# The prologue of a two-layer transformer kernel: tables for four batches first, rounding shared out, FiLM weights in three pieces

## The reference

```python
ln    = (x - mean) / sqrt(var + 1e-5) * ln_g + ln_b
gamma = cond @ Wg.T + bg ;  beta = cond @ Wb.T + bb        # one row for each batch
h     = gamma * ln + beta
q,k,v = h @ Wqkv.T + bqkv                                  # 16 heads of 32
out   = (softmax(q k^T) / sqrt(512)) v ;  out = out @ Wp.T + bp
h1    = out + x ;  x1 = gamma*LN(h1)+beta + h1             # the same gamma, beta
```

## Time and profile before

| what | us |
|---|---|
| median of 3 runs | 1538.35 (1538.13 to 1538.81) |
| the profiled execution, its own time | 1537.32 |
| its span in the profile | 1535.4 |
| TensorE busy in the span | 1515.0 |
| TensorE busy from 0 to 28.67 us | 13.33 |
| first `scores` matmul starts | 53.20 |

### The profile page before, as it was taken

The page is one execution under the profiler, slowest core; times in us unless marked ns, Lnnn a source line. Parts: engine busy times, 40 slices in busy tenths (PEclk is TensorE's granted clock), DMA queues, the critical chain, the costliest instruction groups (busy, mean ns, idle before and its releaser), DMA issues.

```text
span 1535.4 us, 24533 instructions
## 1 busy us (share of the span) xinstructions
PE 1515.0 (99%) x8992; PEld 1235.9 (80%) x8992; DVE 788.4 (51%) x1616; ACT 592.9 (39%) x1884; POOL 581.4 (38%) x504
## 2 busy tenths in 40 slices
PE   5999999999999999999999999999999999999999
PEld 4888888888887668888788888888888888888887
DVE  5677777777766675555546342332524233252522
ACT  4656565656554446555554221211212121121210
POOL 5656666676654545443553311021211102121100
PEclk9999999999999999999999999999999999999999
DMA  7122222222126234333343220020201002020100
GB/s 252 63 80 87 80 93 77 96 77 91 58 81 232 71 138 158 97 103 126 122 127 114 69 69 15 1 82 0 75 7 68 14 1 81 0 75 7 55 1 28
DMA packets 60237, 117.87 MB, mean 77 GB/s; under 512 B 6352, under 2 KB 10448, under 8 KB 60144
## 3 DMA queue, kind: packets, MB, share of 16 engines
q1 hardware_dynamic: 60144, 116.65, 22.4%
HBM read 91.33 MB, written 25.30 MB: 76 GB/s over the span
## 4 chain that ended last, share of the span: by engine, by line
PE 97%; POOL 1%; DVE 1%; DMA 1%; SPq 0%; issue 0%
PE bank L587 27%; PE bank L589 27%; PE bank L588 27%; PE bank L666 4%; PE bank L659 2%; PE bank L677 2%; PE bank L963 2%; PE bank L884 1%; PE bank L718 1%; PE bank L709 1%; PE bank L611 1%; PE bank L987 1%; POOL xa L1746 1%; DMA xa<-xt_in 1%; PE bank L906 1%; PE bank L966 0%
## 5 line engine op out<-in xcount | busy, mean ns | idle before, releaser
L1705 DVE CAST g_hi<-gf 128x512 fp32r<-128x512 f32 x128 | 68.7, 537 | 427.1 <-ACT gf L1271 427.1
L1271 ACT ACTIVATE gf<-bank,cols 128x512 f32<-128x512 f32 x128 | 88.3, 690 | 512.6 <-PE bank L589 512.6
L1106 ACT ACTIVATE pa<-bank,neg_max 128x128 f32<-128x128 f32 x512 | 181.7, 408 | 135.5 <-DVE neg_max L1378 135.5
L587 PE MATMUL bank<-w_hi,g_hi 128*128 128x512 f32 x512 | 200.5, 392 | 0.0
L587 PE MATMUL bank<-hb_hi,w_hi 128*128 128x512 f32 x512 | 199.4, 389 | 0.3 <-DVE vb_lo L1294 0.3
L589 PE MATMUL bank<-w_hi,g_lo 128*128 128x512 f32 x512 | 199.4, 389 | 0.0
L588 PE MATMUL bank<-w_lo,g_hi 128*128 128x512 f32 x512 | 199.2, 389 | 0.0
L589 PE MATMUL bank<-hb_hi,w_lo 128*128 128x512 f32 x512 | 199.2, 389 | 0.0
L588 PE MATMUL bank<-hb_lo,w_hi 128*128 128x512 f32 x512 | 199.2, 389 | 0.0
L1781 POOL TENSOR_TENSOR pa<-pa,rec 128x512 f32<-128x512 f32 x128 | 143.2, 1126 | 56.2 <-DVE rec L1401 56.1
L1755 POOL TENSOR_TENSOR xrc<-xrc,b 128x512 f32<-128x512 f32 x32 | 48.7, 1550 | 303.0 <-DMA xrc<-x_dram 302.9
(11 more groups left out here) (201 smaller groups left out, 3132.6 us busy)
## 6 DMA issues: line engine op xcount, KB each, us to landing
rows<-st_dram SPq DMA_DIRECT2D x32, 512.0 KB, 4.3
xb<-x_dram SPq DMA_DIRECT2D x60, 256.0 KB, 2.9
xa<-xt_in SPq DMA_DIRECT2D x32, 256.0 KB, 4.4
xra<-xt_in SPq DMA_DIRECT2D x32, 256.0 KB, 2.7
x_dram<-h SPq DMA_DIRECT2D x32, 256.0 KB, 2.0
xrb<-x_dram SPq DMA_DIRECT2D x32, 256.0 KB, 3.3
stage_w<-w_in SPq DMA_DIRECT2D x16, 512.0 KB, 3.8
x_dram<-xrb SPq DMA_DIRECT2D x32, 256.0 KB, 2.2
```

What stands on the lines that cost most here:

```text
L587: nc.tensor.matmul(dst, w_hi, a_hi, start=start, stop=False)
L1106: last = nc.scalar.activation(pa[:, j, m, :], scores_bank[j][:, m * P:(m + 1) * P], ACT.Exp, bias=neg_max[:, j * C + m:j * C + m + 1], acc ...
L1271: nc.scalar.activation(gf[f % 2][:], bank[f % 2][:], ACT.Gelu, bias=cols[:, B1_COL + f:B1_COL + f + 1])\
L1705: nc.vector.tensor_copy(g_hi[:, r, :], gf[f % 2][:]).then_inc(g_hi_ready, 1)
```

## The change

Nothing is computed differently; order and engine change.

- SyncE issues the first three x tiles ahead of `cond`, the FiLM weights in three pieces (k = 0 and 1; k = 2; k = 3) with `cols` after the first, the fourth x tile behind them, x tiles 4 to 7 ahead of the bias rows, and waits for Wv's load on the new `wk_first` and on `wa_lo_made` 2 (Wp's: 3).
- VectorE makes first the `st_ln` of batches 0 to 3 alone (`first_tables`, 7 instructions of 128x16), and all the tables (`all_tables`, 8 instructions) only inside the loop at m = 0. `st_made` counts one more. TensorE's 8 transposes of the table (`table_rows`) move to m = 2, and VectorE's `st_rows` copies to m = 1.
- Of the first four batches VectorE rounds the two that it scales, ScalarE the other two; VectorE takes the four low halves after all four are rounded.
- GpSimd splits Wk's first 128 columns; ScalarE rounds Wq's first columns, then the rest of Wk, then of Wq.
- TensorE takes `queries(0, 0)` directly after `first_keys`, and each transpose of the next x tile between keys and queries.
- ScalarE's `copy_k(0, m + 1)` stands ahead of `scale_a(GB + m)`, and behind a wait for all the tables; the splits of Wv and Wp stand one round earlier, at m = 0 and 1, on ScalarE and VectorE.

```diff
+            for t in range(3):
+                load_x(t)
             sp.dma_start(cond[:], cond_t.rearrange("(k p) b -> p k b", p=P)).then_inc(consts_in, 16)
-            for t in range(2):
-                load_x(t)
-            for k in range(2):
+            for k in range(3):
+                piece = wgb_piece(k)
                 for i, w in enumerate((wg_t, wb_t)):
-                    sp.dma_start(wgb[:, i, 2 * k:2 * k + 2], weight(w[2 * k * P:2 * (k + 1) * P, :])).then_inc(wgb_in[k], 16)
-            for t in range(2, GB):
-                load_x(t)
+                    sp.dma_start(wgb[:, i, piece], weight(w[piece.start * P:piece.stop * P, :])).then_inc(wgb_in[k], 16)
+                if k == 0:
+                    sp.dma_start(cols[:], cols_d).then_inc(consts_in, 16)
+            load_x(3)
...
@@ TensorE
+            pe.wait_ge(wa_hi_made, 1)
+            pe.wait_ge(wa_lo_made, 1)
+            queries(0, 0)
+            for m in range(1, C):
+                if m == 1:
                     pe.wait_ge(wa_hi_made, 2)
                     pe.wait_ge(wa_lo_made, 2)
+                pe.wait_ge(k_copied, m)
+                keys(0, m)
+                if m > 1:
+                    pe.wait_ge(n_scaled_act, m + 1)
+                norm_a(GB + m - 1, x_bank)
...
+                if m == 2:
+                    table_rows()
+                pe.wait_ge(q_copied, m)
                 queries(0, m)
...
@@ ScalarE
             for n in range(0, GB, 2):
                 scale_a(n, (vq_bank, None, o_bank)[n])
-            for n in range(GB):
                 round_a(n)
-            split_wa(1)
+            split_wa(1, slice(0, P))
+            split_wa(0, slice(P, D))
+            split_wa(1, slice(P, D))
...
+            copy_k(0, 0)
+            act.wait_ge(st_made, 2)
             for m in range(C):
-                copy_k(0, m)
-                if 0 < m < 3:
-                    split_wa(m + 1)
+                if m + 1 < C:
+                    copy_k(0, m + 1)
                 scale_a(GB + m, x_bank)
                 round_a(GB + m)
+                if m < 2:
+                    split_wa(m + 2)
...
@@ VectorE
+            def first_tables():
+                def four(v):
+                    return cols[:, COL[v]:COL[v] + C].unsqueeze(2).broadcast_to([P, C, GB])
+                ga, be, sh = tmp_a[:, :, 0:GB], tmp_b[:, :, 0:GB], tmp_b[:, :, GB:2 * GB]
+                then(nc.vector.tensor_tensor(ga, ft[:, :, 0, 0, 0:GB], four("bg"), ALU.add))
...
+                nc.vector.tensor_tensor(st_ln[:, 0:GB, C:2 * C].rearrange("p b c -> p c b"), sh, be, ALU.add)\
+                    .then_inc(st_made, 1)
...
+                dve.wait_ge(n_scaled_dve, n // 2 + 1)
+                nc.vector.tensor_copy(h_hi[0][:, :, n * P:(n + 1) * P], h_full(n)).then_inc(hi_ready, 1)
-            split_wa(0, slice(0, P))
             for n in range(GB):
-                norm_low(n)
+                norm_low(n, GB)
+            split_wa(1, 1, slice(0, P))
             var_a(GB)
             mean_var(GB)
             add_eps(GB)
-            split_wa(1, slice(0, P))
-            split_wa(0, slice(P, D))
-            split_wa(1, slice(P, D))
...
+            split_wa(0, 2, slice(P, D))
+            split_wa(1, 3, slice(P, D))
...
             for m in range(C):
                 copy_q(0, m)
+                var_a(GB + m + 1)
+                mean_var(GB + m + 1)
+                add_eps(GB + m + 1)
+                if m == 0:
+                    all_tables()
+                if m == 1:
+                    dve.wait_ge(st0_t, 1)
+                    for i in range(2):
+                        nc.vector.tensor_copy(st_rows[:, i * D:(i + 1) * D], ps_t[i][0:NB, :]).then_inc(st_rows_made, 1)
                 norm_low(GB + m)
-                if m < 3:
-                    var_a(GB + m + 2)
-                    mean_var(GB + m + 2)
-                    add_eps(GB + m + 2)
-                if 0 < m < 3:
-                    split_wa(m + 1)
+                if m < 2:
+                    split_wa(m + 2, m + 4)
...
@@ GpSimd
+            for n in range(GB):
+                norm_a(n)
+            first = slice(0, P)
+            pool.wait_ge(stage_in[0], 16)
+            nc.gpsimd.tensor_copy(wk_hi[:, :, first], stage_a[:, 0, :, first]).then_inc(wk_first, 1)
+            pool.wait_ge(wk_first, 1)
+            nc.gpsimd.tensor_tensor(wk_lo[:, :, first], stage_a[:, 0, :, first], wk_hi[:, :, first].bitcast(F32),
+                                    ALU.subtract).then_inc(wk_first, 1)
```

More of the change, by code:

```diff
@@ L301, in block_pair_kernel @@
         var2_ready, ln2_shifted, x1_ready = sem("var2_ready"), sem("ln2_shifted"), sem("x1_ready")
-        raw_in = [sem(f"raw_in{i}") for i in range(4)]
+        raw_in = [sem("raw_vp_in"), sem("raw_qk_in")]
         film_in = [sem("film_in1"), sem("film_in2")]
@@ L589, in split_product @@
                 return nc.tensor.matmul(dst, w_lo, a_hi, start=False, stop=stop)
[L592 to L605, removed]
             def norm_a(n, dst):
@@ L612, in norm_a, with table_rows @@
                 last.then_inc(n_done, 1)
-            for n in range(GB):
[L615 to L621, removed]
+            pe.wait_ge(consts_in, 32)
+            pe.wait_ge(consts_made, 3)
+            for k in range(C):
+                if k != 1:
+                    pe.wait_ge(wgb_in[max(k - 1, 0)], 32)
+                for i in range(2):
+                    tile = 2 * (k % 2) + i
+                    last = nc.tensor.matmul(ps_s[0][NB * tile:NB * (tile + 1), :], cond[:, k, :], wgb[:, i, k, :],
+                                            start=(k < 2), stop=(k >= 2))
+                if k == 1:
+                    norm_a(0, vq_bank)
+                if k == 2:
+                    norm_a(1, kp_bank)
+            last.then_inc(film_done, 1)
+            pe.wait_ge(film_copied, 1)
+            for c in range(C):
+                last = nc.tensor.transpose(ps_s[1][:, c * P:(c + 1) * P], fv0[:, c * P:(c + 1) * P], ident[:])
+            last.then_inc(film_t, 1)
+            norm_a(2, o_bank)
+            norm_a(3, x_bank)
+            def table_rows():
+                pe.wait_ge(st_made, 2)
+                for i in range(2):
+                    for c in range(C):
+                        last = nc.tensor.transpose(ps_t[i][0:NB, c * P:(c + 1) * P], st_flat[:, i * C + c, :], ident[:])
+                last.then_inc(st0_t, 1)
             def keys(g, m):
@@ L765, in _ @@
             first_keys()
[L766 to L771, removed]
+            pe.wait_ge(wa_hi_made, 1)
[3 more added lines that the diff above has]
+                if m == 1:
                     pe.wait_ge(wa_hi_made, 2)
                     pe.wait_ge(wa_lo_made, 2)
-                if m == 1:
-                    pe.wait_ge(wa_lo_made, 4)
-                wait(pe, q_copied, m)
-                queries(0, m)
[L778 to L783, removed]
+                pe.wait_ge(k_copied, m)
[3 more added lines that the diff above has]
+                norm_a(GB + m - 1, x_bank)
+                if m == 1:
+                    pe.wait_ge(wa_hi_made, 3)
+                    pe.wait_ge(wa_lo_made, 3)
+                if m == 2:
+                    table_rows()
+                pe.wait_ge(q_copied, m)
+                queries(0, m)
+            pe.wait_ge(n_scaled_act, GB + 1)
+            norm_a(2 * GB - 1, x_bank)
+            pe.wait_ge(wa_hi_made, 4)
+            pe.wait_ge(wa_lo_made, 4)
             values(0)
@@ L1055, in _, with split_wa @@
             wa_dst = [wk_hi, wq_hi, wv_hi, wp_hi]
[L1057 removed]
+            def split_wa(i, n=slice(0, D)):
                 act.wait_ge(stage_in[i % 2], 16 * (i // 2 + 1))
[L1059 to L1061 removed]
+                nc.scalar.activation(wa_dst[i][:, :, n], stage_a[:, i % 2, :, n], ACT.Identity).then_inc(wa_hi_made, 1)
             def affine(src, dst, st, free):
@@ L1077, in round_a @@
             def round_a(n):
[L1078 to L1082, removed]
+                act.wait_ge(n_scaled_act, n - 1 if n >= GB else n // 2 + 1)
                 if n >= AHEAD:
@@ L1747, in norm_a @@
                                         ALU.mult).then_inc(xn_ready, 1)
-            for n in range(AHEAD + 1):
+            for n in range(GB):
[6 more added lines that the diff above has]
+                                    ALU.subtract).then_inc(wk_first, 1)
+            for n in range(GB, AHEAD + 1):
                 norm_a(n)
```

82 lines of the change are left out of this document (43 added, 39 removed).

## The result

| | median, us | range | runs |
|---|---|---|---|
| before | 1538.34 | 1536.59 to 1539.08 | 15 |
| changed | 1541.39 | 1540.19 to 1542.57 | 15 |

The ratio is 1.0021, 95% interval 1.0013 to 1.0029: the kernel became slower by some 3 us, where the prediction said 1.3 us for the likeliest case, with a range of 1536.0 to 1542.4. The profiled execution took 1541.47 us, close to its median. That of before (1537.32) lay 1.0 under its own, so the two profiles differ by 4.15 us and the medians by 3.05.

A forecast was written before the change was run, and what follows sets the result against it. TensorE's own work was taken to bound everything behind 28.67 us, so only the scores' start moves: 17.0, 16.45, 7.65 and 13.4 give 54.5 against 53.2, +1.3 us, median 1539.7; range 1536.0 to 1542.4.

The forecast's parts named there:

- the head start: First tables ready sooner: about 3 us, used up by the pause before block 1's queries are copied, tile 6 and eight transposes.
- Rival 3: Head start absent: weights held back or small table steps dear, M1 18.6 to 19.2, +1.6 to +2.2 us, 1541.6; chance 0.07.
- rival 5: VectorE's tables wait for GpSimd's tile: +1.9 us, 1541.6; chance 0.04.
- M1: Moment the first tables are ready: 17.0 us, bounds 16.5 and 18.6, against 19.24 before.
- M1 to M2: From first tables to all tables ready: rounding, low halves, Wq and Wk splits, queries copy, statistics, tables; 16.45 us.
- M2 to E: From all tables ready until VectorE has copied block 1's queries, behind Wv's rounding and low half: 7.65 us.
- The pause: TensorE stands still ahead of `queries(0, 2)` until VectorE has copied block 1's queries: 2.5 us.
- E to the scores: From VectorE's copy of block 1's queries to the first scores: 13.4 us, including a 1.3 us pause for tile 6.
- What should cost nothing: Work taken as covered, chiefly GpSimd's two steps for Wk's first columns, 2.31 us each, done at 20.0 and 22.3.
- The rule weighed: Shared port pair as exclusive lock: VectorE's two-SBUF-operand table steps would wait out GpSimd's tile 5; not used in the sum.
- Rival 2: The pause ahead of `queries(0, 2)` lowers TensorE's clock: up to 1.5 us more, 1541.2; chance 0.09.
- Rival 1: No pause ahead of `queries(0, 2)` and the gain stays: 2.4 us faster, median 1536.0; chance 0.13.

The follow-up runs named there:

- unread matmuls: Changed kernel plus five float32 matmuls of 128x512, result read by nobody, in TensorE's idle time ahead of the first keys: 1540.95 us, ratio 1.0016.
- the loop's order: Changed kernel with VectorE's low halves of Wv and Wp one block later, behind the copy of the next block's queries: 1538.26 us, ratio 1.0003.
- the kernel where TensorE had no pause behind it: Changed kernel with first tables for eight batches, VectorE's low halves one block later, and FiLM matmuls of k = 2 and 3 together: 1536.80 us, ratio 0.9991.

## Why the prediction was right or wrong

The direction and the mechanism were right: the head start of the first tables is lost again to a pause ahead of `queries(0, 2)`. The size was 1.3 us and is 3.05 in the medians, 4.7 in the profiles' scores. The median lies at the upper edge of the forecast's own span (1541.4) and close to the 1541.6 of rivals 3 and 5, so the number alone could not choose between them; the rows do. Step by step:

- *M1: the term that failed.* Foretold 17.0, found 19.4. The prediction went straight from the landing of the last weights (12.6; found 12.5) to the last two FiLM matmuls, as if TensorE stood ready. It did not: by the written order the transposes of tile 0 ran until 12.8, the pair of k = 2 took 1.92 us, for a pair costs as much as a set, and the transposes of tile 1 another 1.0. So the last pair started at 15.60, 3.1 us behind the landing. Its own price, 1.05 us for the foretold half of 1.94, came out by luck: 1.94 is four matmuls at the slow pace of the early prologue, and at full speed four take 1.06, so two are not half. Some 0.5 us came back between `fv0`'s copy and the first table step (1.35 for 1.86), and 0.2 in the seven short steps (1.32 for 1.5). Rival 3 had named 18.6 to 19.2 for M1, with causes (late weights, dear small steps) that the traces refute.
- *M1 to M2.* 17.4 for 16.45. The missing 0.9 is VectorE's wait for the first queries, 0.92 in its row. It comes from the first keys at half clock, for with the full clock the wait is gone. The prediction had let the first keys take 4.25 us at the slow clock, as they had before, and so took it for covered; all twelve were slow this time, and they took 5.26.
- *M2 to E.* 7.57 for 7.65. *The pause*: 2.42 for 2.5. *E to the scores*: 13.6 for 13.4, with the pause of 1.30 at tile 6 (1.3 foretold). The reading of the written order, term by term, held to 0.2 us.
- *What should cost nothing.* GpSimd's two steps took 0.61 and 1.27 us, under the 2.31 taken, were done in time, and held nothing up in the changed kernel's profile. But the prediction asked only when they end, not what they hold up: where they meet the table steps they cost up to 1.1 us in other profiles.
- *The rule weighed.* In the sum and in rival 5 VectorE was not to be held by GpSimd's normalising step, and the 1.9 us of rival 5 did not come: all the tables took 3.05 us, from 33.68 to 36.73, for the foretold 2.93. Under GpSimd's step for tile 5 (34.52 to 36.60) the first long step with two SBUF operands took 0.46 us and the next two 0.28 and 0.29, so none waited for GpSimd's end. The copy behind them took 0.74 us (0.38 before) and ended 0.13 behind GpSimd's step; whether it was held is open. GpSimd's subtraction and its cast did hold such steps to their end. So the second half of the rule in "SBUF — State Buffer" of the Trainium skill, on the shared port pair, agrees with these runs for GpSimd's cast and subtraction, and not for its normalising step.
- *Rival 2*, a slow clock behind the pause, did not come in the changed kernel's profile: the clock read 1.00 from 44 us on, behind 2.42 us of idle time. It did come in the same kernel with unread matmuls, behind 2.52 us, at the price foretold (1.5 us), most of which the pause at tile 6 would have taken anyway. Which of the two the other executions met is not known.
- *Rival 1*, no pause and the gain kept, is half of what the loop's order alone does: the pause is gone, but the median is 1538.3 and not 1536.0, for M1 was late and 0.91 us at tile 7 were left.

The rows for the rule weighed, GpSimd and then VectorE, both of the changed kernel:

```profile
34.52 2.08 POOL L1781 TENSOR_SCALAR xa<-xa,mv,rstd 128x512 f32<-128x512 f32 x1
```

```profile
34.96 0.46 DVE L1364 TENSOR_TENSOR st_flat<-tmp_a,cols 128x128 f32<-128x128 f32 x1
```

## What to carry to other kernels

When a step leaves the path and is put into a queue written out by hand, follow what stands behind it on every engine that waits for it: here the tables cost nothing themselves, and their place ahead of Wv's rounding, with Wv's low half ahead of a copy of queries, cost 2 to 3 us. Ask the same of the engine that is to use the data: that it has landed says nothing of what stands ahead on that engine. Splitting a load into finer pieces pays only if the work on a piece is itself divisible, and these FiLM matmuls, which fill four column strips together, were not. The pause ahead of the first keys was paid twice, once as idle time and once as slow clock. Filling it with unread matmuls won 1.5 to 1.9 us in the kernel where TensorE had no pause behind it; in the kernel before (1.0 us) and in the changed one (0.4) the gain in the median was not clear of nothing.

## What the runs showed of the hardware

- Two float32 matmuls of 128x512 onto 32-column strips took 1.05 us, four took 1.06.
- Early in the prologue the same instructions run at about half speed: four transposes 1.12 and later 0.66 us, a pair of FiLM matmuls 1.92 and later 1.05, though the granted clock is shown as 1.00 in both stretches. Where the slow pace ends differs from one execution to the next: the pair of k = 2, at 12.8 us in the changed kernel, took 1.92 there and 1.29 in the profile of the loop's order. That this is the slow clock, not yet in the records, is argued and not shown. "TensorE: Matmul & The Clock Gate" of the Trainium skill, in its part on the clock gate, says that throttled is the default state and activity releases it, which would fit; no row here can tell.
- A VectorE step with two SBUF operands took 1.29 us in place of 0.21 and ended 0.07 behind a GpSimd subtraction of two SBUF operands (17.51 to 18.83); another took 0.65 in place of 0.19 and ended 0.04 behind a GpSimd cast of one SBUF operand (16.82 to 17.43). Under GpSimd's one-operand normalising step, of 2.08 us or more, such steps took 0.28 to 0.66 and did not wait for its end.
- Nearly the same idle time does not always bring the slow clock: behind 2.42 us at 42 us the clock stayed at 1.00, behind 2.52 us at 41 us in the changed kernel with unread matmuls it fell to 0.50 for some 3 us.
